# First chunk of a two-FFN-plus-attention kernel: eight up projections ahead of most gates, gated values written over the gate's bank, all weight pieces loaded at once, the next chunk's routing five units later

## What is computed

```python
def ffn(x):                      # x: 2048 x 128
    shared = silu(x @ Ws_up) @ Ws_down
    aff = x @ centroids.T        # 2048 x 64 experts
    idx = top_k(aff + expert_biases, 8)
    w = sigmoid(aff[idx]); w = w / (sum(w) + 1e-8)
    h = silu(einsum('td,edf->etf', x, W_up))      # 64 experts, 128 -> 64
    y = einsum('etf,efd->etd', h, W_down)
    return shared + sum over chosen experts of w * y
x = x + 0.5 * ffn(layernorm(x))
x = x + attention(layernorm(x))
x = x + 0.5 * ffn(layernorm(x))
```

## Time and profile before

| | |
|---|---|
| time, median of 3 runs | 545.74 us (545.43 to 548.09) |
| profiled execution | 545.78 us, of which the span is 544.0 us |
| TensorE (PE) busy | 533.0 us, 98% of the span |
| ScalarE (ACT) busy | 407.3 us, 75% |
| VectorE (DVE) busy | 407.0 us, 75% |
| GpSimd (POOL) busy | 274.0 us, 50% |

### The profile page before, as it was taken

One profiled execution on the slowest core, in us unless ns is written; L12 is line 12 of the kernel. 1 busy time (PEld: TensorE's weight loads), 2 busy tenths in 40 slices (PEclk: granted clock), 3 DMA queues, 4 the chain that ended last, 5 costly groups with the idle time before them and its releaser, 6 DMA issues.

```text
span 544.0 us, 8636 instructions
## 1 busy us (share of the span) xinstructions
PE 533.0 (98%) x2679; PEld 435.0 (80%) x2679; DVE 407.0 (75%) x926; ACT 407.3 (75%) x814; POOL 274.0 (50%) x242
## 2 busy tenths in 40 slices
PE   8899999999999999999999999999999999999997
PEld 5577887887888887699999999777887888788885
DVE  5989679877976676767777889778677867866564
ACT  6899778877887776766666667678778777877774
POOL 3579767775776763000000000166675776766663
PEclk9999999999999999999999999999999999999999
DMA  7676565554565540000000000055555565656562
GB/s 259 182 215 194 184 195 161 179 189 159 173 187 196 189 157 1 1 1 1 1 2 1 1 1 1 16 195 168 174 202 159 175 194 179 176 166 201 198 189 92
DMA packets 44270, 72.25 MB, mean 133 GB/s; under 512 B 8864, under 2 KB 9632, under 8 KB 44224
## 3 DMA queue, kind: packets, MB, share of 16 engines
q1 hardware_dynamic: 43568, 71.17, 41.9%
q10 hardware_dynamic: 592, 0.39, 0.2%
q0 software_dynamic: 64, 0.13, 0.1%
HBM read 69.57 MB, written 2.10 MB: 132 GB/s over the span
## 4 chain that ended last, share of the span: by engine, by line
PE 88%; DVE 6%; ACT 2%; issue 2%; DMA 1%; SPq 0%; DVEq 0%
PE lrow L1064 13%; PE lrow L1065 13%; PE lrow L1066 13%; PE bank L1102 11%; PE bank L1104 11%; PE bank L1103 11%; PE bank L1136 6%; PE bank L1348 3%; PE bank L1350 2%; PE bank L1349 2%; DVE pmax L879 1%; PE bank L1143 1%; PE bank L1064 1%; PE bank L1065 1%; PE bank L1066 1%
## 5 line engine op out<-in xcount | busy, mean ns | idle before, releaser
L277 POOL TENSOR_TENSOR gpart_lo<-gated,gpart_hi 128x512 fp32r<-128x512 f32 x174 | 224.0, 1296 | 164.2 <-ACT gpart_hi L442 162.5
L431 ACT ACTIVATE lrow<-lrow 128x512 f32<-128x512 f32 (+1 forms) x246 | 144.4, 587 | 63.9 <-PE lrow L1066 63.5
L678 DVE TENSOR_TENSOR gated<-lrow,wide 128x512 f32<-128x512 f32 x170 | 116.3, 684 | 57.6 <-ACT lrow L431 56.3
L442 ACT CAST gpart_hi<-gated 128x512 fp32r<-128x512 f32 x174 | 106.7, 613 | 5.7 <-DVE gated L678 5.1
L1102 PE MATMUL bank<-gpart_lo,wdn_hi 128*128 128x512 f32 x256 | 101.7, 397 | 0.0
L1104 PE MATMUL bank<-gpart_hi,wdn_hi 128*128 128x512 f32 x256 | 101.4, 396 | 0.0
L1103 PE MATMUL bank<-gpart_hi,wdn_lo 128*128 128x512 f32 x256 | 101.1, 395 | 0.0
L678 DVE TENSOR_TENSOR lrow<-lrow,wide 128x512 f32<-128x512 f32 x74 | 51.5, 696 | 28.0 <-ACT lrow L431 28.0
L997 DVE TENSOR_TENSOR pT_lo<-bank,pT_hi 128x512 fp32r<-128x512 f32 x64 | 43.8, 685 | 24.2 <-ACT pT_hi L618 24.2
L277 DVE TENSOR_TENSOR gpart_lo<-lrow,gpart_hi 128x512 fp32r<-128x512 f32 (+1 forms) x84 | 57.3, 682 | 1.8 <-ACT gpart_hi L442 1.3
L1102 PEld LDWEIGHTS bank<-gpart_lo,wdn_hi 128*128 128x128 f32 x256 | 48.0, 188 | 11.8
(11 more groups left out here) (246 smaller groups left out, 944.2 us busy)
## 6 DMA issues: line engine op xcount, KB each, us to landing
wide<-gates_dram SPq DMA_DIRECT2D x488, 128.0 KB, 3.0
raw<-in_w_up SPq DMA_DIRECT2D x8, 256.0 KB, 6.1
raw<-in_w_down SPq DMA_DIRECT2D x8, 256.0 KB, 6.3
gates_dram<-gates SPq DMA_DIRECT2D x8, 128.0 KB, 2.3
x<-in_x SPq DMA_DIRECT2D x3, 256.0 KB, 3.7
out_dram<-x SPq DMA_DIRECT2D x3, 256.0 KB, 3.0
x<-in_x SPq DMA_DIRECT2D x1, 128.0 KB, 2.7
x<-in_x ACTq DMA_DIRECT2D x1, 128.0 KB, 2.9
```

Source lines behind the costliest of these rows:

```text
L277: return eng.tensor_tensor(gpart[1][0:m, U % NGP, :], gated_at(U)[0:m, :], gpart[0][0:m, U % NGP, :].bitcast(F32), ALU.subtract)
L431: nc.scalar.activation(dst[0:m, :], hid[U % NH][0:m, :], ACT.Silu).then_inc(s_silu, 1)
L442: nc.scalar.copy(gpart[0][0:m, U % NGP, :], gated_at(U)[0:m, :]).then_inc(s_ghi, 1)
L678: nc.vector.tensor_tensor(gated_at(U), a, b, ALU.mult).then_inc(s_gated, 1)
```

## The change

All of it concerns the first chunk (n = 0); `when(n, first, usual)` gives another place to a step there and leaves it elsewhere.

- TensorE makes ups 0 to 5 before `pro_cw` and up 6 behind it, without `stay_awake`; ups 7 to 10 are mixed with the six spread gates and downs 0 to 5, and the loop starts at unit 11 (`LEADS` 11).
- The gated values of units 1 to 6 go into the bank of their gate, not into `hid`, so ups 4 to 10 wait only for the silu of the unit four before; the spread of a gate waits for the low part of the unit two before instead of its gate.
- The low part of unit 0 moves to GpSimd, `sel` from ScalarE to VectorE, the reciprocal of the first routing into PSUM, two small splits (`pad_lo`, and the value weights) from before the first gate to units 11 and 12.
- All 16 weight pieces are loaded up front, in another order (`STEPS`).
- The next chunk's routing stands at later units: `pro_xT` 8 to 14, `pro_hi` 9 to 15, `pro_lo` 9 to 14, `joint_product` 11 to 17, `joint_turn` 13 to 19, `pro_aff` 13 to 18, and so on to `pro_cw` 24 to 27; the store of its gates from unit 30 to 32.

```diff
-PRE = 3
-FIRST = 12
-LEADS = (4, 4)
+PRE = 2
+STEPS = (0, 2, 1, 4, 3, 6, 5, 8, 7, 10, 9, 12, 11, 14, 13, 15)
+FIRST = 16
+LEADS = (11, 4)
 WARM = 5
...
-                return u > EARLY and u % 2 == 1
+                return u == 0 or u > EARLY and u % 2 == 1
...
+            if 1 <= U <= EARLY:
+                return gate[(U + 1) % 2]
...
-            w = (wup[part], flat(wdn[part]))[k % 2]
-            return w[:, (k // 2) * PW:(k // 2 + 1) * PW]
+            i = STEPS[k]
+            w = (wup[part], flat(wdn[part]))[i % 2]
+            return w[:, (i // 2) * PW:(i // 2 + 1) * PW]
+
+        def split(i):
+
+            return STEPS.index(i) + 1
+
+        def first_unit(n, at):
+
+            return at if n == 0 else min(n % NCH, 1)
...
-                if k == 5:
+                if k == 1:
                     load_x(1)
...
-                    if u == STORE and n % NCH != NCH - 1:
+                    if u == when(n, UNITS - 1, STORE) and n % NCH != NCH - 1:
...
                             piece_lo(k)
-                    for u in range(min(c, 1), UNITS):
+                        low_part(nc.gpsimd, 0).then_inc(s_glop, 1)
+                        piece_lo(PRE + 1)
+                        piece_lo(PRE + 2)
+                        rstd(0, 1, p_st, p_rs)
+                        piece_lo(PRE + 3)
+                    for u in range(first_unit(n, EARLY + 1), UNITS):
                         if on_pool(place(u, n)):
                             low_part(nc.gpsimd, place(u, n)).then_inc(s_glop, 1)
                         if n == 0 and u % 2 == 0 and PRE + u // 2 < 2 * WP:
@@ -406,9 +428,9 @@
...
+                            if u == when(n, 22, 18):
                                 weights(n + 1)
-                            if u == 21:
+                            if u == when(n, 25, 21):
                                 normed_weights(n + 1)
...
-                dst = hid[U % NH]
+                dst = hid[U % NH] if U else gated_at(U)
...
-                            nc.scalar.copy(small[0][:, E + F:LOADED], raws[:, E + F:LOADED]).then_inc(s_wh, 1)
                             nc.scalar.copy(wsdn[0][:, :], rawd[:, :]).then_inc(s_wh, 1)
-                            act.wait_ge(s_spread, 1)
-                            make_sel()
+                            piece_hi(1)
                             act.wait_ge(f_bias, 1)
                             nc.scalar.activation(flat(sil), bank[0][:, 0:TPC * E], ACT.Sigmoid).then_inc(p_sil, 1)
                             nc.scalar.activation(eps[:, 3:4], eps[:, 0:1], ACT.Silu)
-                            piece_hi(1)
                             silu_unit(0, n)
                             silu_unit(1, n)
                             hi_unit(0, n)
                             silu_unit(2, n)
                             piece_hi(2)
+                            act.wait_ge(p_cwT, 1)
+                            nc.scalar.copy(cwT[:, :], mp[:, :]).then_inc(p_cwr, 1)
+                            silu_unit(3, n)
                             pro_cwT(n)
-                            silu_unit(3, n)
...
-                            if u == 9:
+                            if u == when(n, 15, 9):
                                 pro_hi(n + 1)
-                            if u == 12:
+                            if u == when(n, 18, 12):
...
+                        if n == 0 and u == EARLY + 3:
+                            nc.scalar.copy(small[0][:, E + F:LOADED], raws[:, E + F:LOADED]).then_inc(s_wh, 1)
+                        if n == 0 and u == 16:
                             turned_hi()
...
+            def first_sel():
+
+                dve.wait_ge(s_spread, 1)
+                cols = spread[:, 0:2 * EARLY].bitcast(F32).rearrange("p (i e) -> p i e", e=2)
+                nc.vector.tensor_copy(sel[:, :, :, :], cols.unsqueeze(3).to_broadcast([P, EARLY, 2, F])).then_inc(s_sel, 1)
...
-                inv = wsum[:, 1, :].unsqueeze(2).to_broadcast([P, TPC, E])
+                inv = (wsum[:, 1, :] if n else bank[0][:, TPC * (E + 1):TPC * (E + 2)]).unsqueeze(2).to_broadcast([P, TPC, E])
...
                             first_lo(1)
+                            first_sel()
                             first_top()
                             first_chosen()
                             dve.wait_ge(s_zero, 1)
                             first_weights(n)
-                            small_lo(1, small, raws, E + F, LOADED)
-                            small_lo(2, wsdn, rawd, 0, D)
-                            lo_unit(0, n)
-                            pad_lo()
-                    for u in range(min(c, 1), UNITS):
+                            small_lo(1, wsdn, rawd, 0, D)
+                            dve.wait_ge(s_x[1], 16)
+                            raw_stats(0, 1, (0, 1))
+                            stats(0, 1, p_st, (2, 3))
+                            gate_unit(1, n)
+                            gate_unit(2, n)
+                            lo_unit(1, n)
+                            gate_unit(3, n)
+                            lo_unit(2, n)
+                            lo_unit(3, n)
+                            gate_unit(4, n)
+                            gate_unit(5, n)
+                            lo_unit(4, n)
+                            lo_unit(5, n)
+                            gate_unit(6, n)
+                    for u in range(first_unit(n, EARLY + 1), UNITS):
                         gate_unit(u, n)
-                        if c or u > 1 - f:
+                        if c or f and u or u > EARLY:
                             lo_unit(*before(u, n))
                         if c + 1 < NCH:
                             if u == min(c, 1):
                                 if f == 0:
                                     dve.wait_ge(s_x[c + 1], 16)
                                 raw_stats(0, c + 1, (0, 1))
-                            if u == 2:
+                            if n and u == 2:
                                 stats(0, c + 1, p_st, (2, 3))
-                            if u == 5:
+                            if u == when(n, 8, 5):
                                 normed(0, n + 1, c + 1, xn[f], p_rs, p_xn, (0, 1))
-                            if u == 6:
+                            if u == when(n, 9, 6):
                                 normed(0, n + 1, c + 1, xn[f], p_rs, p_xn, (2, 3))
...
-                            if u == 15:
+                            if u == when(n, 20, 15):
...
+                        if n == 0 and u == 11:
+                            pad_lo()
+                        if n == 0 and u == 12:
+                            small_lo(2, small, raws, E + F, LOADED)
...
-                    pe.wait_ge(s_w, 2 * ((u - 1) // (PAIRS // WP)) + 1)
-                if U >= NH:
+                    pe.wait_ge(s_w, split(2 * ((u - 1) // (PAIRS // WP))))
+                if NH <= U <= NH + EARLY:
+                    pe.wait_ge(s_silu, U - NH + 1)
+                elif U >= NH:
                     wait_hid_free(pe, U - NH)
...
                 if early_unit(u, n):
-                    if u > 2:
+                    if u > 2 and n:
                         pe.wait_ge(s_gated, nth_gated(u - 2, n))
+                    elif u > 2:
...
                             up(u, n)
-                        stay_awake(2)
                         pro_cw(n)
-                        stay_awake(1)
-                    if c == 0:
-                        pe.wait_ge(p_cwr, f + 1)
-                    for u in range(min(c, 1), UNITS):
-                        if u <= EARLY and (c or u >= LEADS[f]):
+                        up(6, n)
+                        pe.wait_ge(p_cwr, 1)
+                        spread_gate(1, n)
+                        spread_gate(2, n)
+                        up(7, n)
+                        down(0, n)
+                        spread_gate(3, n)
+                        up(8, n)
+                        down(1, n)
+                        spread_gate(4, n)
+                        up(9, n)
+                        spread_gate(5, n)
+                        down(2, n)
+                        up(10, n)
+                        spread_gate(6, n)
+                        down(3, n)
+                        down(4, n)
+                        down(5, n)
+                    elif c == 0:
+                        pe.wait_ge(p_cwr, 2)
+                    for u in range(first_unit(n, LEADS[0]), UNITS):
+                        if n == 0 and u <= LEADS[0] + 1 or u <= EARLY and (c or u >= LEADS[f]):
                             up(u, n)
-                        if u > EARLY and u % 2 == 1:
+                        elif u > EARLY and u % 2 == 1:
...
-                        if n or u != 3:
-                            spread_gate(u, n)
+                        spread_gate(u, n)
                         if u > LAG or u == LAG and c == 0:
                             down(u - LAG, n)
                         elif c:
@@ -1278,13 +1355,13 @@
```

85 lines of the change are left out of this document (50 added, 35 removed).

## The result

| | before | after |
|---|---|---|
| median | 545.42 us (545.01 to 548.25, 20 runs) | 547.11 us (546.69 to 548.65, 20 runs) |
| profiled execution | 545.78 us, span 544.0 | 547.95 us, span 546.1 |

The ratio is 1.0023, with a 95% interval of 1.0013 to 1.0034: 1.3 us slower by the ratio, 1.7 by the medians, and inside the 0.5% that the prediction called no change.

What follows compares the result with a forecast made beforehand. TensorE bounds the kernel, its early waits capping gains at 7.6 us; VectorE paces it after the front. A 4.4 us lead, less later waits, plus 1.3 of old waits, ends 1.0 us later: 546.7 median, range 543.0 to 548.8.

Steps and rivals of the forecast that it cites:

- rival 1: VectorE takes back the lead TensorE gains at the front: within 1.7 us of 546.7, chance 0.58.
- lead at up 11, less the transposes' 0.65: First chunk's front: TensorE reaches this point at 24.67 instead of 29.69 us, 4.4 us ahead without the next input's transposes.
- up 12: TensorE, free at 26.07, waits for VectorE's low part 8 until 28.32: 2.25 us of the lead lost.
- ups 22, 24, 26: TensorE waits behind VectorE's late routing steps: 0.7, 1.6 and 0.4 us, 2.7 in all.
- small restarts, and the waits that before has itself: Between 29.69 and 58.02 us: minus 0.3 for restarts, plus 1.3 for waits already in the kernel before.
- Two new waits of VectorE: Later routing leaves VectorE idle before `pro_lo` (at least 1.2, 1.7 us with silu 15) and `pro_aff` (at least 1.5, likely 2.35).
- The router: First routing's product falls from 0.80 to some 0.2 us with the reciprocal in PSUM; `pro_cw` can start at 13.95, not 14.44.
- Gates from DRAM: Unit 7's broadcasts land at 23.3 to 24.1 us, gate 7 wants them at 23.70: 0 to 0.4 us, taken as 0.
- Rival 4: Broadcasts of gates land late behind the weight pieces, delaying VectorE from unit 7: 549.2 at 2.5 us late, chance 0.10.
- Rival 5: TensorE's clock falls to 1.2 GHz behind the wait at up 12; ten matmuls cost 2.3 us more: 549.0, chance 0.04.
- rival 2: Part of the front's lead stays, with cheaper splits and VectorE's two waits at their least: 544.5 or 543.5, chance 0.15.
- rival 3: All or most of the front's 4.4 us lead stays, VectorE doing units 7 to 26 without waits: 541.3 to 543, chance 0.13.

Runs made afterwards that it cites:

- experiment 10: The changed kernel with the reciprocal of the first routing back in SBUF: 548.18 us, ratio 1.0050.
- experiment 7: The kernel before with only the reciprocal of the first routing put in PSUM: 544.67 us, ratio 0.9971.
- experiment 1: The changed kernel plus six idle TensorE matmuls of 128x256 between down 6 and up 12: 547.84 us, ratio 1.0038.
- experiment 2: The changed kernel with VectorE's steps of the next chunk's routing, sum included, one unit later: 545.61 us, ratio 0.9993.
- experiment 5: Changed kernel repeated: 547.09 us; and with VectorE's routing one unit later, sum kept at unit 24, GpSimd's `normed_weights` moved from 25 to 24: 545.12 us.
- experiment 8: The changed kernel with the next chunk's routing up to top 8 four units later than before on all engines: 543.73 us, ratio 0.9964.
- experiment 6: Experiment 5's one-unit-later kernel with both halves of the next chunk's norm also one unit later (9 and 10): 545.54 us, ratio 0.9993.

## Why the prediction was right

The forecast was 546.7 us, no measurable change, by rival 1: VectorE takes the lead back. The time was 547.11. Its terms, in the order of the sum, with two traces beside them: the changed kernel's, which has the slow stretch, and experiment 10's, the same kernel but for one operand, at full clock:

| term | predicted | changed kernel | experiment 10 |
|---|---|---|---|
| lead at up 11, less the transposes' 0.65 | 4.4 | 4.2 (29.69 - 0.65 - 24.86) | 4.1 (up 11 at 24.95) |
| up 12 | 2.25 | 2.05 | 2.06 |
| up 14 | 0.4 | none | 0.27 |
| up 18 | 0.8 | 0.73 | 0.73 |
| ups 22, 24, 26 | 2.7 | 2.1 (0.41 + 1.37 + 0.32) | 2.1 |
| `pro_cw` | 0.25 | 0.45 | 0.44 |
| small restarts, and the waits that before has itself | 1.0 gained | 0.1 (what is left) | 0.4 gained (what is left) |
| slow stretch behind up 12 | none (chance 0.04) | 1.1 on the path | none |

Measured waits are the step to that start less a matmul's 0.234. In experiment 10's trace they add to 5.6 us, which is 1.5 more than the lead; up 29 is 1.1 later than before (59.10 against 58.02), so 0.4 was given back. In the changed kernel's trace the slow stretch covers the wait of up 14, and what it leaves in the last-but-one row is less certain.

The term that was sized wrong is the one given back. The sum takes 1.3 us of waits from the trace of before. Two of them are waits: the steps to up 18 (40.05 to 40.64) and up 22 (46.45 to 46.97) are 0.36 and 0.29 us over a matmul's. The rest are first matmuls behind a wait or a group of small ones, 0.1 us each, and the changed kernel has these too. The row of up 18 in the trace of before:

```profile
...
40.64 0.50 PE L1064 MATMUL lrow<-xnT_lo_a,wup_hi 128*128 128x512 f32 x1 [0.19 <-DVE gpart_lo L277]
```

**Where VectorE is.** Hand-laid times were met to 0.02 us: gate 6 at 23.11 for 23.10, gate 7 at 23.71 for 23.70, low part 8 at 27.58 for 27.57, up 12 at 28.31 for 28.32. From gate 6 on this needed only the hand-over times of the earlier trace rows. That it agrees to the hundredth is luck. At the front the whole trace runs some 0.4 us ahead by an earlier start: the reduction before the first sum stands at 11.74, in the trace of before at 12.14, but at 12.00 in the repeat of the changed kernel and at 11.84 in experiment 7's, where nothing ahead of it was edited. So gate 1 is at 15.43 for 15.73, and by low part 2 (18.80 for 18.85) most of that was lost again. The repeat has up 12 at 28.57.

**Two new waits of VectorE.** Forecast 1.7 and 2.35 us, measured 2.78 and 2.38. The first is 1.1 too long, and that is the clock: in the traces of experiments 1 and 10 it is 1.65 and 1.60. That the waits cost time behind 33 us was a main step of the argument, and experiments 2 and 5 show it: putting VectorE's steps one unit later gives 1.5 to 2.0 us back. In experiment 8, with neither wait, the whole is 3.4 faster. The other main step, the wait of up 12, is the largest term. The trace shows it, released by low part 8; no experiment takes it away.

**The router.** The product costs 0.20 as said, but for another reason than given: the earlier trace rows show it against a split that stands elsewhere in the changed kernel (experiment 10). The rule and the row were right; that the collision would still be there was not asked. The 0.5 us that the prediction gave the edit comes from the order of the new lists: experiment 10 goes without the edit and has the same times at full clock. In the kernel before, the same edit is worth 1.0 (experiment 7). The splits at units 11 and 12 took 0.31 and 0.70, 1.0 us together where the sum had 1.1.

**Gates from DRAM.** No wait, as taken, although the broadcasts were issued 0.5 us later than before. Rival 4 falls.

**The clock.** Rival 5 had a chance of 0.04, which was too little. Its mechanism came in the changed kernel's trace and in its repeat's; by the mean clock 10 of the 31 executions are below 0.999, and these have a median 1.1 us above the others. It cost 1.1 us on the path, half of the 2.3 that the rival gave it. It does not decide the verdict. At full clock the changed kernel has 546.9 against 545.5, or 1.4 us for the 1.0 forecast, and the traces without the slow stretch have up 29 at 59.09 and 59.10 where the forecast had 59.0. That this agrees to 0.1 is partly luck. The waits were put at 0.8 us too much in all (6.4 for 5.6), the lead at 0.3 too much, and the 1.0 that was to be given back was 0.4; the errors cancel.

The kernel before loses its full clock too, in 15 of 85 executions, in 11 of them with a mean of 0.993 or 0.994. The prediction read full clock in every slice from one trace. No trace shows where the kernel before loses it.

**Rivals 2 and 3**, part or all of the lead kept, did not come with this change, but rival 3's mechanism is in reach. Experiment 8 keeps 2.6 us of the lead at up 29. What bounds it, by the trace, is VectorE from 22 to 33 us, busy 10.58 of 11.00 us there too; experiment 6 shows that shifting the norm moves the wait on.

**The range.** The text says that 543.0 to 548.8 takes in the near half of rival 3, which reaches only up to 543, and it gives its chance for slower than 548.5 where the range ends at 548.8. The result lies far from both ends.

## What to carry to other kernels

A lead of one engine is worth only what the engine behind it can follow; lay out that engine's list by hand with hand-over times from the trace before you count the lead. When a pipeline of small steps is moved across engines, move every engine's steps by the same number of units and look at what each reader stands behind: one unit of difference cost 1.5 to 2.0 us here, as much as the change as a whole. And measure the small edits of a large change by themselves: the one that takes a collision away was worth 1.0 us by itself and nothing inside the large change, which had moved the other party away.
